# Router logits of the first layer with the router's weights as the loaded operand, in four quarters, and one transpose

## The reference

```python
x = x + 0.5 * ffn0(layernorm(x))        # mixture of 8 experts, 2 chosen
x = x + mamba(layernorm(x))
x = x + 0.5 * ffn0(layernorm(x))        # the same weights again
x = x + 0.5 * ffn1(layernorm(x))
x = x + attention(layernorm(x))
x = x + 0.5 * ffn1(layernorm(x))

def ffn0(x):
    gate = einsum('bsd,de->bse', x, W_gate)             # router logits, 128 -> 8
    kth = top_k(gate, 2)[0][..., -1:]
    mask = softmax(where(gate >= kth, gate, -inf))
    h = relu(einsum('bsd,edh->bseh', x, W1) + b1)       # 128 -> 512
    y = einsum('bseh,ehd->bsed', h, W2) + b2            # 512 -> 128
    return (y * mask[..., None]).mean(axis=-2)
```

## Time and profile before

| what | us |
|---|---|
| median of 3 timed runs | 1909.24 |
| their lowest and highest | 1908.29, 1911.15 |
| span of the profiled execution | 1950.7 |
| TensorE busy in it | 1767.5 (91%) |
| VectorE, GpSimd, ScalarE busy | 1251.3, 1205.6, 1097.7 |
| mean granted TensorE clock | 0.974 of full |

### The profile page before, as it was taken

How to read it: one execution, slowest core, us unless ns; L and a number is a source line. 1 busy time by engine, 2 the same in 40 slices (tenths; PEclk the granted TensorE clock), 3 DMA queues, 4 the chain that set the end, 5 groups by cost and what they waited for, 6 DMA issues and landing times. The chain is left out here.

```text
span 1950.7 us, 35578 instructions
## 1 busy us (share of the span) xinstructions
PE 1767.5 (91%) x12105; PEld 1514.1 (78%) x12105; DVE 1251.3 (64%) x2922; ACT 1097.7 (56%) x1929; POOL 1205.6 (62%) x1197
## 2 busy tenths in 40 slices
PE   7999998999999989986889988888899999988898
PEld 6888776777777868765678867777799999967777
DVE  2358888697886867879894445333576767554333
ACT  3466666666666666665655452433577677552342
POOL 3138787677777768779995443555455555444553
PEclk9999999999998999998999998999899999999999
DMA  4023333232233223322332200112553454001113
GB/s 143 1 77 109 107 99 104 84 100 91 90 98 99 90 83 103 104 83 74 103 93 68 81 30 31 40 43 69 166 147 119 135 153 135 12 33 33 44 43 99
DMA packets 120509, 166.66 MB, mean 85 GB/s; under 512 B 13814, under 2 KB 55756, under 8 KB 120332
## 3 DMA queue, kind: packets, MB, share of 16 engines
q1 hardware_dynamic: 113292, 148.79, 25.1%
q0 software_dynamic: 7040, 15.60, 2.6%
HBM read 114.14 MB, written 50.20 MB: 84 GB/s over the span
## 5 line engine op out<-in xcount | busy, mean ns | idle before, releaser
L789 POOL TENSOR_TENSOR db<-du_m,bt 128x512 f32<-128x512 f32 x256 | 327.5, 1280 | 147.6 <-DVE bank L794 147.1
L794 DVE TENSOR_TENSOR_SCAN bank<-bank,db 128x512 f32<-128x512 f32 x256 | 312.6, 1221 | 17.3 <-ACT bank L779 17.2
L820 POOL TENSOR_TENSOR y_m<-y_m,ph 128x512 f32<-128x512 f32 x240 | 312.8, 1304 | 0.4 <-DVE ph L809 0.4
L779 ACT ACTIVATE bank<-dt_m,a_neg 128x512 f32<-128x512 f32 x256 | 176.1, 688 | 86.2 <-DVE ph L809 80.0
L809 DVE TENSOR_TENSOR ph<-bank,ct 128x512 f32<-128x512 f32 x240 | 166.0, 692 | 8.6 <-POOL y_m L820 0.5
L1304 POOL TENSOR_TENSOR s_a<-s_a,mx_a 128x768 f32<-128x768 f32 x64 | 94.1, 1470 | 86.3 <-DVE mx_a L1387 86.3
L1418 PE MATMUL bank<-vb_a,pT_a 96*128 96x64 f32 x1024 | 121.6, 272 | 0.0
L1418 PEld LDWEIGHTS bank<-vb_a,pT_a 96*128 96x128 f32 x1024 | 119.7, 192 | 0.0
L359 PEld LDWEIGHTS bank<-dn,hf2b 128*128 128x128 f32 x680 | 91.4, 196 | 16.6 <-DVE x_all L418 6.7
L359 PEld LDWEIGHTS bank<-dn,hf1b 128*128 128x128 f32 x680 | 90.2, 194 | 17.5 <-DVE x_all L418 7.8
L359 PEld LDWEIGHTS bank<-dn,hf0b 128*128 128x128 f32 x688 | 91.3, 194 | 10.2 <-DVE x_all L418 2.4
(11 more groups left out here) (463 smaller groups left out, 4877.7 us busy)
## 6 DMA issues: line engine op xcount, KB each, us to landing
bt<-bc_rows SPq DMA_DIRECT2D x128, 256.0 KB, 3.5
ct<-bc_rows SPq DMA_DIRECT2D x128, 256.0 KB, 3.4
sorted<-zero_row SPq DMA_DIRECT2D x64, 288.0 KB, 4.0
k_strips_a<-k_rows SPq DMA_DIRECT2D x32, 256.0 KB, 3.1
q_strips_a<-q_rows SPq DMA_DIRECT2D x32, 256.0 KB, 3.8
q_rows<-q_hi_a SPq DMA_DIRECT2D x16, 256.0 KB, 3.1
q_rows<-q_lo_a SPq DMA_DIRECT2D x16, 256.0 KB, 3.3
k_rows<-k_hi_a SPq DMA_DIRECT2D x16, 256.0 KB, 3.2
```

The lines of the kernel that those rows point to most:

```text
L779: eng.activation(DH[J % 2][:], dt[s % 2][:, j % NH, :], ACT.Exp, scale=a_neg[:, j % NH, j // NH:j // NH + 1]).then_inc(da_done.sem)
L789: eng.tensor_tensor(db[J % RD][:], du[s % 2][:, j % NH, :], bt[N % RB][:], ALU.mult).then_inc(db_done.sem)
L794: eng.tensor_tensor_scan(DH[J % 2][:], DH[J % 2][:], db[J % RD][:], 0.0, ALU.mult, ALU.add).then_inc(hs_done.sem)
L820: eng.tensor_tensor(y[s % 2][:, j % NH, :], y[s % 2][:, j % NH, :], ph[J % RP][:], ALU.add).then_inc(ys_done.sem)
```

## The change

The router's weights, padded with zeros from 8 to 32 columns, become the loaded operand, and the tokens stream through. Each block of 128 tokens gives a 32x128 result in its own quarter of the partitions of `XB`. ScalarE copies the 128x128 to a new tile `gT`, TensorE turns it with one transpose, and VectorE reads 8 of every 32 columns. On TensorE this is a third piece of the preparation; all slots are laid out anew. At the start the router's weights get a semaphore of their own and are loaded behind the first biases, after the memset of their tile. The diff, with the long declarations cut:

```diff
@@ ffn0_up
-    W = dict(..., wg=sb("wg", [P, E]), ...)
-    W["small"], W["b2_ld"], W["b2_zero"] = S.dma("f0_small_loaded", 1, ("wg", "b1")), S.dma("f0_b2_loaded", NT), S.count("f0_b2_zeroed")
+    W = dict(..., wg=sb("wg", [P, QB]), ...)
+    W["small"], W["wg_ld"], W["b2_ld"], W["b2_zero"] = S.dma("f0_b1_loaded"), S.dma("f0_gate_loaded"), S.dma("f0_b2_loaded", NT), S.count("f0_small_zeroed", 1, ("wg", "b2"))
...
     def sync_small(eng):
-        eng.dma_start(W["wg"][:], w["gate"]).then_inc(W["small"].sem, 16)
         eng.dma_start(W["b1_rows"][:], w["b1"]).then_inc(W["small"].sem, 16)
 
-        eng.wait_ge(W["b2_zero"].sem, W["b2_zero"].at(0))
+        eng.wait_ge(W["b2_zero"].sem, W["b2_zero"].at(0, "b2"))
+        eng.dma_start(W["wg"][:, 0:E], w["gate"]).then_inc(W["wg_ld"].sem, 16)
         for k in range(NT):
             eng.dma_start(W["b2"][k * E:(k + 1) * E, k * D:(k + 1) * D], w["b2"]).then_inc(W["b2_ld"].sem, 16)
@@ ffn0
+    gT = sb("gT" + tag, [P, P])
-    pa = S.count(n + "_prep_act", NSEQ, ("out", "xT", "hi", "exp"))
+    pa = S.count(n + "_prep_act", NSEQ, ("out", "xT", "hi", "gT", "exp"))
-    pp = S.count(n + "_prep_pe", NSEQ, ("T", "gate"))
+    pp = S.count(n + "_prep_pe", NSEQ, ("T", "gate", "turned"))
-    PREP_PE, PREP_ACT, PREP_POOL = (25, 27), (24, 25, 25, 28), (23,)
-    PREP_DVE = (22, 22, 25, 27, 27, 27, 27, 29, 29, 29, 29)
+    PREP_PE, PREP_ACT, PREP_POOL = (24, 26, 28), (23, 24, 24, 26, 30), (22,)
+    PREP_DVE = (21, 21, 24, 29, 29, 29, 29, 31, 31, 31, 31)
@@ prep_pe
         if s == 0:
-            eng.wait_ge(W["small"].sem, W["small"].at(0, "b1"))
+            eng.wait_ge(W["wg_ld"].sem, W["wg_ld"].at(0))
         XB.wait(eng)
         for k in range(NT):
-            x = eng.matmul(XB.psum[:, k * E:(k + 1) * E], xT[:, k * P:(k + 1) * P], W["wg"][:], start=True, stop=True)
+            x = eng.matmul(XB.psum[k * QB:(k + 1) * QB, 0:P], W["wg"][:], xT[:, k * P:(k + 1) * P], start=True, stop=True)
         x.then_inc(pp.sem)
+        XB.free = (pa.sem, pa.at(s, "gT"))
+        yield
+        XB.wait(eng)
+        eng.transpose(XB.psum[:, 0:P], gT[:], C["ident"][:]).then_inc(pp.sem)
         XB.free = (pd.sem, pd.at(s, "lg"))
         yield
@@ prep_act, behind the copy to xT_hi
+        if s >= 1:
+            eng.wait_ge(pp.sem, pp.at(s - 1, "turned"))
+        eng.wait_ge(pp.sem, pp.at(s, "gate"))
+        eng.copy(gT[:], XB.psum[:, 0:P]).then_inc(pa.sem)
+        yield
@@ prep_dve
-        eng.wait_ge(pp.sem, pp.at(s, "gate"))
-        eng.tensor_copy(lg[:], XB.psum[:, 0:NT * E].rearrange("p (k e) -> p k e", e=E)).then_inc(pd.sem)
+        eng.wait_ge(pp.sem, pp.at(s, "turned"))
+        eng.tensor_copy(lg[:], XB.psum[:, 0:P].rearrange("p (k e) -> p k e", e=QB)[:, :, 0:E]).then_inc(pd.sem)
@@ front
         def dve(eng):
+            eng.memset(W["wg"][:], 0.0).then_inc(W["b2_zero"].sem)
             eng.memset(W["b2"][:], 0.0).then_inc(W["b2_zero"].sem)
...
         def pe(eng):
-            eng.wait_ge(W["small"].sem, W["small"].at(0, "b1"))
+            eng.wait_ge(W["small"].sem, W["small"].at(0))
```

More of the change, by code:

```diff
@@ L185, in ffn0_up @@
 def ffn0_up(nc, S, sb, w):
-    W = dict(up_hi=sb("up_hi", [P, E, HID], F32R), up_lo=sb("up_lo", [P, E, HID], F32R), dn=sb("dn", [P, E, HC, D]), wg=sb("wg", [P, E]),
+    W = dict(up_hi=sb("up_hi", [P, E, HID], F32R), up_lo=sb("up_lo", [P, E, HID], F32R), dn=sb("dn", [P, E, HC, D]), wg=sb("wg", [P, QB]),
              b1=sb("b1", [P, E, HC]), b1_rows=sb("b1_rows", [E * HC, P]), b2=sb("b2", [NT * E, NT * D]))
-    W["small"], W["b2_ld"], W["b2_zero"] = S.dma("f0_small_loaded", 1, ("wg", "b1")), S.dma("f0_b2_loaded", NT), S.count("f0_b2_zeroed")
+    W["small"], W["wg_ld"], W["b2_ld"], W["b2_zero"] = S.dma("f0_b1_loaded"), S.dma("f0_gate_loaded"), S.dma("f0_b2_loaded", NT), S.count("f0_small_zeroed", 1, ("wg", "b2"))
     W["raw_ld"] = [S.dma(f"f0_raw{r}_loaded", 2) for r in range(4)]
@@ L231, in ffn0 @@
     xT_lo = [sb(f"xT_lo{p}" + tag, [P, SEQ], F32R) for p in range(2)]
-    lg, top = sb("lg" + tag, [P, NT, E]), sb("top" + tag, [P, NT, 8])
+    gT, lg, top = sb("gT" + tag, [P, P]), sb("lg" + tag, [P, NT, E]), sb("top" + tag, [P, NT, 8])
     sel, ex, den = sb("sel" + tag, [P, NT, E]), sb("ex" + tag, [P, NT, E]), sb("den" + tag, [P, NT])
```

## The result

The change is faster: 1905.49 us against 1909.15 us before, medians of 18 runs each, a ratio of 0.9972 with a 95% interval of 0.9961 to 0.9984.

A forecast was written before the change was run, and what follows sets the result against it. TensorE, 92% busy from 290 to 740 us, was taken as the bound. Gate and turn 3.2, earlier slots 2.7, start 0.5 and VectorE's wait -0.3 made +6.1 us on 1909.24: 1915.3 us, range 1907 to 1920.

The forecast's parts named there:

- Step 1: Gate products on TensorE: eight records without overlap, 1.13 us against 0.89, so +0.24 us a sequence.
- the lower bound, 0.71: Least gate cost on TensorE a sequence: seven steps of 43 ns, one stream, 0.30 us for entry and exit.
- Step 2: The turn on TensorE: one transpose record for each sequence, two slots after the gate, +0.11 us each.
- The count of 9 of 16: Of 16 sequences' inserted TensorE time, 9 count in full, the rest absorbed in waits; +3.2 us for gate and turn.
- Step 3: Earlier preparation slots: TensorE waits 1.4 us at chain a's sequence 1, 1.3 at chain b's sequence 7; +2.7 us.
- Step 4: The start: bias load earlier, -0.5 us, but longer gate, copy and turn before the first up product; +0.5 us net.
- Step 5: The rest: VectorE's 14.3 us of gate waiting mostly goes, but it then waits for down products; -0.3 us.
- the sign named for a wrong forecast: The forecast is wrong if VectorE's 194.3 us of waiting for down products changes by more than 10.
- rival D: Slower: ScalarE's stand at the gate and copy delay the decay 0.7 us at 14 sequences; 1925.1 us, chance 0.07.
- Rival C: Faster: all eight gate records overlap and half of VectorE's 14.3 us gate wait comes back; 1903.6 us, chance 0.15.
- I am wrong if the gate's slot is shorter than 2.4: Sign against the forecast: TensorE's slot with the gate, forecast at 2.7 us, comes out below 2.4 us.

The follow-up runs named there:

- whole_array: The changed kernel with the router's weights in zero-padded 128-column tiles, the four gate products accumulating through the whole array; ratio 1.0010 to the kernel before, 1.0002 when run again.
- gate_twice: The kernel before with each sequence's four gate products issued twice; 1925.84 us, ratio 1.0090 to the kernel before.
- slots_early: The kernel before with every piece of the preparation one slot earlier, gate products as before; 1957.52 us, ratio 1.0078 to the kernel before.
- act_out: The kernel before, but ScalarE copies the logits out of the bank and VectorE reads them two slots later; 1905.18 us, ratio 0.9986 to the kernel before.
- lg_at_turn: The changed kernel with VectorE reading the logits one slot earlier, in the turn's own slot; 1909.60 us, ratio 1.0019 to the kernel before.
- psum_choice: The changed kernel without VectorE's copy of the logits: maximum, choice and subtraction read straight from the bank; 1900.21 us, ratio 0.9965 to the kernel before.
- transposes_later: The changed kernel with statistics, scale, normalization and transposes back in the earlier kernel's slots, one later; 1902.72 us, ratio 0.9971 to the kernel before.

## Why the prediction was wrong

**Step 1, the gate's products: wrong in sign.** Charged were 8 records at 0.11 us, with 0.25 for entry and exit: 1.13 us. Measured are 0.55 us (2.14 less 1.59). The step took its row from the 40-column records, as the nearest by width. Those go one after the other through the same columns of the array, and so do the 16 records of the earlier trace rows. Neither shows what records in four different quarters do, and the text said so, and then took no overlap as the likeliest. Even the lower bound, 0.71, was too high. It stepped the records by 43 ns, the pitch of records to one quarter, where four now start 7 ns apart and only one step, between the two fours, is 113 ns: all eight starts lie in 0.15 us, not in 0.30. Its 0.30 for entry and exit was right, 0.29 measured. The failed term is the eight streams in a row, 0.88 us in the forecast, in whose place the starts and the last stream take 0.26. So the gate costs 0.34 us less than before and not 0.24 more: a difference of 0.58 us, 9 us over 16 sequences. Of the 11.4 us between forecast (+6.1) and measurement (-5.3), 7.3 are this term's as it stood in the sum (9 x 0.24 forecast, 15 x -0.34 measured). This is the failure that turned the sign; `whole_array` shows it by itself.

The Trainium skill's rule ("TensorE: Matmul & The Clock Gate", Part 3: Packing small matmuls), that tiles in different column groups run concurrently with starts some 4 ns apart, holds here with 7 ns. Its page "TensorEngine Tiling (Array Packing)", Key Properties, says that a change of mode drains the engine; the 0.29 us of entry and exit agree with it, and the price is small against the gain. The mask's transpose, which also loads 32 columns, pays none of it: it starts 111 ns behind the last down product, and the up product 29 ns behind it.

**Step 2, the turn: right.** Forecast +0.11 us a sequence, measured 0.10 to 0.11.

**The count of 9 of 16: wrong.** `gate_twice` prices the time at all 16, the start's included. A discount for sequences in which TensorE waits anyway finds no support; why those in 740 to 1055 us count too was not tested.

**Step 3, the early slots: right where it was worked out.** 1.4 and 1.3 us forecast, 1.33 and 1.30 measured, at the two sequences named. Sequences 2 to 4 of chain a, "-1 to +1 for all", came to +0.25, -0.21 and +1.45, above the bound; two sequences of chain b, which the step didn't name, gave 1.3 us back. All waits at the transposes together rose by 2.8 us, so that the term of +2.7 fits them partly by luck. `slots_early` shows the first of these waits without the change. What the step lacks is that a wait of some microseconds can bring a stretch at half clock behind it, as at 203.95 us there.

**Step 4, the start: wrong in sign, for the same reason.** +0.5 forecast, -0.97 measured. The earlier load gave 0.42 as forecast (0.5); the gate was counted as 1.84 us plus extras, and lasts 0.65.

**Step 5, VectorE's wait: right in what happens, too small in what it is worth.** That the 14.3 us go was forecast; the sum took 0.3 us for it. `act_out` gives 2.7 (0.8 to 4.8), `lg_at_turn` more. In the trace of `act_out` it is 13 us up to the place where one copy stands 5.32 us, so the 2.7 hold a loss that the prediction had nowhere: that a VectorE instruction can stand behind several of GpSimd's. The argument, that VectorE would only wait for the next down product instead, holds for a third: in `act_out` its wait for the down products rose from 194.3 to 199.0 us, 4.7 of the 14.6 that went at the logits. In the change it fell to 186.4; the sign named for a wrong forecast, over 10 us there, did not come. ScalarE's stand at the gate is 9.9 us in all (5.8 for `gTb` and 4.1 for `gTa`, 12 times), and it costs nothing that the runs show; rival D had priced it at 9.8 us.

**The sum by the measured sizes:** gate at 15 sequences 15 x -0.34 = -5.1; turn 15 x 0.11 = +1.7; the start with sequence 0, -1.0; the two early waits +2.6; VectorE's wait -2.7. Together -4.5 us, against -5.3 measured (-7.4 to -3.1). The agreement is better than its terms. VectorE's -2.7 is net of the stand in `act_out` and comes with an interval of 2 us to either side, and the gate's and the turn's terms are only 3.4 us less for TensorE, whose busy time falls by 8.6 in the two traces. That rest can't be assigned to an edit. The clock does not explain it: up to chain b's sequence 4 the kernel after has 20 us at half clock and before 34, which could be 7 us, but behind it it has more, and over the whole front it is 68 against 65. `act_out` and `psum_choice`, which take VectorE's wait away, have little of it in the first stretch (24 and 17), and `lg_at_turn` and `gate_twice`, which have the wait, more (37 and 34); but `transposes_later`, which has no such wait, has 37, and one kernel traced twice had 37 and 24. So part of what VectorE's wait is worth may come through the clock, and that is argued, not shown.

Rival C had the time, 1903.6 (1909.24 less 5.3 is 1903.9), with a chance of 0.15, but not its terms: it took -0.6 for gate and turn, where -3.4 is measured, and -7.2 for VectorE, where -2.7 is. Its time was right by luck. "I am wrong if the gate's slot is shorter than 2.4" was the sentence that told it.

## What to carry to other kernels

Small products that use a quarter of the array's columns, each to its own quarter of the partitions, cost here far less than one after the other: 0.55 us for four products in two records each, of which entry and exit are 0.29, where whole-array products took 0.89. A row of narrow records through the same columns says nothing about that, so where the disputed price decides the sign, hold both branches as cases of near equal weight. A reader that stands early in a strict queue holds what is behind it: let it read some slots behind the producer, as `act_out` shows for a kernel with its own gate. And follow the lead over the old kernel along the trace: the change was 15.6 us ahead at one point and lost 5.9 of them where a single short instruction stood for 4.3 us. `psum_choice`, made to take that loss away, only moved it.

## What the runs showed of the hardware

- **VectorE held by GpSimd for several instructions.** An instruction of 0.19 us with two operands in SBUF stood 4.30 us in the change, 5.38 in `psum_choice`, while GpSimd ran its products of 1.3 us back to back, and it ended 0.05 us behind one of them. The same befell a copy from SBUF to SBUF in `act_out` (5.32 us). Instructions beside it with an operand in the bank were not held (1.22 us for each scan and 0.69 for each product, with GpSimd running). The Trainium skill ("SBUF — State Buffer", Terms) says that the two share a port pair that is taken for a whole instruction and blocks the loser; the rows agree. That the loser can miss three or four turns in a row, and that moving one such instruction only handed the wait to the next, is what these runs add.
- **The clock around a wait.** Round waits of TensorE of some microseconds (4.20 us at 203.95 in `slots_early`, 2.59 at 258.75 in `transposes_later`, 5.94 at 1000.59 and 2.10 at 849.63 in the change) the granted clock fell to the lower of the two levels, 1.2 GHz, for 3.4 or 6.8 us, so such a wait can cost more than its length. It doesn't always: 2.83 us before 200.55 in the kernel before and 2.70 us before 251.18 in the change were followed by full clock, as was every wait of 1.3 us shown here. The length does not decide it: in the second trace of the change the same wait of 2.70 us, before 251.30, had 3.4 us at 1.2 GHz with it.
- **Two waves of four.** The second four records start 133 ns after the first four, 113 ns after the last of them, while each record lasts 272 to 297 ns.
